# A mixture-of-experts stage whose first weight matrices are read per tile and whose second product is made of three fp32r products

## The chip, the cores and the metric

The kernel runs on one core of a Trainium2 chip. Work is done by five engines, each with an instruction queue of its own: TensorE (PE in the rows; its weight loads are PEld), VectorE (DVE), ScalarE (ACT), GpSimd (POOL) and SyncE (SP, which issues most DMAs). They meet through semaphores. The metric is the device time of one launch in microseconds; lower is better.

## What is computed

A pre-LN decoder layer on x of shape (8, 256, 256): attention with Gaussian scores, then cross-attention with 16 heads, then a mixture of eight experts, each added to x. Only the last part is touched:

```python
gate_logits = xs @ Wg                                   # xs: layernorm of x, (2048, 256)
weights, sel = jax.lax.top_k(gate_logits, 2)
weights = jax.nn.softmax(weights, axis=1)
h = jax.nn.relu(jnp.einsum('td,edf->etf', xs, W1) + b1[:, None, :])      # W1: (8, 256, 1024)
out_e = jnp.einsum('etf,efd->etd', h, W2) + b2[:, None, :]               # W2: (8, 1024, 256)
out = jnp.einsum('tk,tkd->td', weights, picked)         # the two chosen rows of out_e
```

## The kernel before

Each engine runs an order that is written out by hand. The attention part is a loop over the batches, software-pipelined: `attention` runs iterations -1 to 9, and in each of them the engines do pieces of up to four batches. Iterations 8 and 9 (`choosing` and `placing`) also route the first ten token tiles: `routing_table(0, 0..3)` builds in four rounds on VectorE the one-hot operands (`row_hot`, L1711, and three `tile_vals`, L1719) for the matmuls that make the table of slots, and `routing_index` turns the table into gather indices.

The expert part is a loop over 39 tiles of 128 slots, sorted by expert, in iterations n = 0 to 42, the first 18 unrolled. In iteration n GpSimd gathers the rows of tile n (L1876) and scatters tile n-4 into the output in HBM (L1890); TensorE transposes tile n-1 (`ex_rows_t`, L1901), makes the hidden layer of tile n-2 (`ex_hidden`, L1933, 16 fp32 matmuls, two records each) and the second product of tile n-3 (`ex_out`, L1966, 8 fp32 matmuls of 256 columns). ScalarE copies the transposed rows (L1907) and does four relus (L1952); VectorE copies W1 of the tile's expert out of the resident weights (`ex_weights`, L1918, 128x2048), does the other four relus (L1945), and adds the bias and multiplies by the routing weight (L1978, L1980). Each engine first reads the tile's expert from a table (`value_load`, L1852).

The first 13 tiles come from the first ten token tiles. The remaining six token tiles are routed on VectorE within iterations 3 to 12, after the tile's own work: the choice in 3, counts in 4, fillers and tile lists in 5, fillers and slots in 6, four table rounds in 7 to 10, and the index in 12. GpSimd can gather tile 13 (iteration 13) only after that index.

W1 and W2 of all experts, 16 MB, are kept in SBUF (`experts_w`). SP loads them expert by expert, one pair of 1 MB transfers after the other: expert 0 early, 1 in iteration 8, and from the fourth on after the last batch's heads are transposed (`p_hT`, L927).

Of the kernel before, what the change touches and what calls it, by code (L numbers as in the profile page):

```python
# [31 lines left out]
NB = 8  # L32
# [14 lines left out]
PLACE = KT * FF + FT * D  # L47
EARLY = 1
QROWS = 2 * 3 * HD
# [8 lines left out]
UNROLLED = 18  # L58

# [124 lines left out]
def run(core):  # L184
# [16 lines left out]
    for name, (engine, setup, finish) in programs.items():  # L201
        @engine
        def _(eng, name=name, setup=setup, finish=finish):
# [4 lines left out]
            if name != "sync":  # L208
                pipeline(eng, MAX_TILES, MOE_LAG, lambda it: experts(core, name, eng, it), first=UNROLLED)
# [15 lines left out]
def plan_memory(core):  # L225
# [22 lines left out]
    core.experts_w = buffer(core, "experts_w", [NE * PLACE])  # L248


def plan_shared(core):
    sb = partial(buffer, core)
    core.ident = sb("ident", [P])
    core.ones = sb("ones", [P])
    core.x2 = sb("x2", [TT, D])
# [5 lines left out]
    core.tile_loads = sb("tile_loads", [MAX_TILES + 1], I32)  # L261
# [76 lines left out]
def plan_late_experts(core, late_end):  # L338
    sb = partial(buffer, core)
    core.hid_t = [sb(f"hid_t{i}", [FT, P]) for i in range(2)]  # L340
# [74 lines left out]
    core.w1_now = [sb(f"w1_now{i}", [KT * FF]) for i in range(2)]  # L415
    end, core.cursor = core.cursor, start
# [16 lines left out]
def make_events(core):  # L433
# [3 lines left out]
    for n in "x_first0 x_first1 x_rest consts_first consts_in weights weights_value weights_cross weights_last mask_in experts_in experts_b residual_out".split():  # L437
        E[n] = sem(core, n)
# [20 lines left out]
    for n, k in per.items():  # L459
# [3 lines left out]
              "vec pool both filler filled prefix counted delta ex slots table tabled idx b1_in b1_t".split()}  # L463
    core.rows_in = RowsIn([sem(core, f"rows_in{i}") for i in range(4)])
    core.rows_out = dma_event(core, "rows_out")
    per = dict(gnow=1, snow=1, xT=1, slots_t=1, w1=1, hid=2, act_a=4, act_v=4, b1t=1,
# [239 lines left out]
def attention(core, name, eng, it):  # L706
# [14 lines left out]
    if name == "sync":  # L721
        if it.v == 1:
            for x in range(EARLY):
                load_expert(core, eng, x, core.E["experts_in"])
# [40 lines left out]
    exps(2, 2, 3, 4)  # L765
    at(0, st_rbf_out)
# [8 lines left out]
    exps(2, 8, 9)  # L775
    at(0, st_normalise, 1)
# [46 lines left out]
    at(2, st_transpose, "hT")  # L823
    scores(0, 0, 1, 2)
# [526 lines left out]
def store_residual(core, eng, b):  # L1351
    core.e["x2"].wait(eng, b)
    loads(core, eng, core.out.rearrange("b (t p) d -> b p t d", p=P)[b.v], x2_of(core, b), core.E["residual_out"])
# [41 lines left out]
def experts_sync(core, e):  # L1395
    t, r = core.t, core.r
    core.e["av"].wait(e, LAST_BATCH.back(1), 3)
    load_expert(core, e, EARLY, core.E["experts_in"])
# [9 lines left out]
def experts_rest_sync(core, e):  # L1408
    for x in range(EARLY + 1, NE):
        if x == EARLY + 2:  # L1410
            core.e["p_hT"].wait(e, LAST_BATCH)
        load_expert(core, e, x, core.E["experts_in"])


def load_expert(core, eng, x, sem):
    if x > 0:
        eng.wait_ge(sem, 32 * x)
    place = core.experts_w[:, (NE - 1 - x) * PLACE:(NE - x) * PLACE]
# [606 lines left out]
```

## Time and profile before

| | |
|---|---|
| median of 3 runs | 663.25 us (663.2 to 665.27) |
| profiled execution | 661.92 us, span 660.2 us |
| mean granted TensorE clock | 0.981 of full speed |
| PE busy | 613.9 us, 93% of the span |
| DVE, ACT, POOL busy | 395.3, 226.1 and 196.6 us |
| HBM read | 29.93 MB |

The span runs from the first to the last instruction of the profiled execution; the remaining 1.7 us of its time lie around it. Busy shares are means over stages that have different limits. The attention part fills the first 350 us, and the expert loop the rest.

### The profile page before, as it was taken

The numbers are of one execution on the slowest core, as the hardware profiler recorded it, in microseconds if no ns is written. First come the engines' busy times: TensorE is split into PE (matmuls) and PEld (weight loads), VectorE is DVE, ScalarE is ACT, GpSimd is POOL, SyncE is SP. The second block draws the span as 40 slices with busy tenths as digits, with TensorE's granted clock in tenths as the row PEclk, the third lists the DMA queues.
The fourth block names the chain that finished last, engine by engine and source line by source line (L and its number), as shares of the span: only waits on it lengthen the run. The fifth ranks groups of instructions, "written<-read, shape, count | busy, mean of one in ns | idle before, by whom it ended". The sixth has DMA issues, their size and how long they took to land.

```text
span 660.2 us, 14238 instructions
## 1 busy us (share of the span) xinstructions
PE 613.9 (93%) x4587; PEld 549.6 (83%) x4588; DVE 395.3 (60%) x1069; ACT 226.1 (34%) x537; POOL 196.6 (30%) x259
## 2 busy tenths in 40 slices
PE   4676999999999999998897999999999999999992
PEld 4576888888898988886676989999999999999992
DVE  4636848677686767676896477765344444544440
ACT  5332373645545373634252111112121221222120
POOL 8312120212012030101005134545345444444422
PEclk9979999999999999998989999999999999999997
DMA  7294818090642809082096883212222222222221
GB/s 219 93 147 120 89 23 92 2 125 23 76 72 37 110 5 141 3 92 71 7 338 200 256 252 96 33 26 48 42 33 32 38 41 32 33 38 40 32 25 16
DMA packets 46996, 52.80 MB, mean 80 GB/s; under 512 B 5920, under 2 KB 43648, under 8 KB 46944
## 3 DMA queue, kind: packets, MB, share of 16 engines
q1 hardware_dynamic: 37936, 41.08, 31.2%
q0 software_dynamic: 7616, 10.26, 9.9%
q10 hardware_dynamic: 1392, 0.79, 0.4%
q8 instruction: 30, 0.49, 0.3%
q14 instruction: 22, 0.18, 0.1%
HBM read 29.93 MB, written 9.31 MB: 59 GB/s over the span
## 4 chain that ended last, share of the span: by engine, by line
PE 80%; DVE 9%; DMA 3%; ACT 3%; issue 2%; POOL 1%; SPq 1%; DVEq 1%; POOLq 0%
PE bank L1933 20%; PE bank L1966 19%; PE bank L961 13%; PE bank L1287 4%; PE bank L1255 4%; PE bank L1198 4%; PE bank L1258 4%; PE bank L1201 4%; PE bank L927 2%; DMA q_stack<-cq_lo 1%; PE bank L1901 1%; PE bank L1097 1%; DMA exp_ring<-L_attn_Wo 1%; DVE row_max L1209 1%; DVE tile_vals L1719 1%
## 5 line engine op out<-in xcount | busy, mean ns | idle before, releaser
L1933 PE MATMUL bank<-slots_t,w_now 128*128 128x128 f32 x1248 | 146.0, 275 | 0.9 <-DVE w_now L1918 0.6
L1933 PEld LDWEIGHTS bank<-slots_t,w_now 128*128 128x128 f32 x1248 | 142.5, 192 | 1.6 <-DVE w_now L1918 1.6
L1966 PE MATMUL bank<-experts_w,hid_t 128*128 x624 | 141.2, 380 | 0.0
L1966 PEld LDWEIGHTS bank<-experts_w,hid_t 128*128 128x128 f32 x624 | 115.7, 190 | 14.1
L1890 POOL DMA_INDIRECT out<-y,scatter_now x39 | 70.8, 1816 | 137.2 <-DVE y L1980 121.2
L1952 ACT ACTIVATE hid_t<-bank,b_tile 128x128 f32<-128x128 f32 x156 | 44.6, 368 | 169.5 <-DVE b_tile L1939 169.5
L1209 DVE TENSOR_REDUCE row_max<-bank 128x2 f32<-128x512 f32 x128 | 81.1, 681 | 10.8 <-PE bank L1201 10.6
L1270 ACT ACTIVATE exp_ring<-bank 128x512 f32<-128x512 f32 x128 | 67.8, 605 | 30.1 <-PE bank L1258 30.0
L1918 DVE COPY w_now<-experts_w 128x2048 f32 x39 | 47.8, 1227 | 49.3 <-issue 41.5
L1201 PE MATMUL bank<-k_stack,q_stack 96*128 96x256 f32 x256 | 68.1, 380 | 0.0
L1258 PE MATMUL bank<-q_stack,k_stack 98*128 98x256 f32 x256 | 67.3, 383 | 0.0
L1978 DVE TENSOR_TENSOR y<-bank,b_row 128x256 f32<-128x256 f32 x39 | 16.5, 424 | 79.1 <-PE bank L1966 74.6
L1258 PEld LDWEIGHTS bank<-q_stack,k_stack 98*128 98x128 f32 x256 | 51.4, 201 | 3.6
L1201 PEld LDWEIGHTS bank<-k_stack,q_stack 96*128 96x128 f32 x256 | 50.7, 198 | 3.6
L1198 PE MATMUL bank<-mask_q,ident_bf 128*128 128x512 bf16 x128 | 50.3, 393 | 2.2 <-DMA q_stack<-cq_lo 2.2
L1255 PE MATMUL bank<-mask_k,ident_bf 128*128 128x512 bf16 x128 | 51.0, 398 | 0.0
L1876 POOL DMA_INDIRECT slots_in<-xn_rows,gather_now x39 | 42.7, 1095 | 26.5 <-POOL gather_now L1873 16.1
L860 POOL TENSOR_SCALAR rstd<-moments 128x2 f32<-128x2 f32 x24 | 5.9, 246 | 144.6 <-DVE moments L857 144.6
L1945 DVE TENSOR_SCALAR hid_t<-bank,b_tile 128x128 f32<-128x128 f32 x156 | 43.9, 344 | 7.9 <-DVE b_tile L1939 4.6
L1907 ACT ACTIVATE slots_t<-bank 128x256 f32<-128x256 f32 x39 | 15.0, 385 | 59.9 <-PE bank L1901 59.9
L1287 PE MATMUL bank<-exp_ring,v_aug 128*32 128x256 f32 x512 | 34.1, 385 | 0.0
L1873 POOL COPY gather_now<-gather_idx 128x1 uint32 x39 | 26.8, 687 | 15.5 <-DVE jump L1763 15.5
(266 smaller groups left out, 937.2 us busy)
## 6 DMA issues: line engine op xcount, KB each, us to landing
experts_w<-L_ffn_W SPq DMA_DIRECT2D x16, 1024.0 KB, 7.7
k_stack<-ck_hi SPq DMA_DIRECT2D x32, 128.0 KB, 4.7
q_stack<-cq_hi SPq DMA_DIRECT2D x32, 128.0 KB, 6.6
ctx_in<-ctx SPq DMA_DIRECT2D x8, 256.0 KB, 8.0
k_stack<-ck_lo SPq DMA_DIRECT2D x16, 128.0 KB, 4.6
q_stack<-cq_lo SPq DMA_DIRECT2D x16, 128.0 KB, 8.1
out<-x SPq DMA_DIRECT2D x7, 256.0 KB, 8.1
xn_rows<-xn_ffn SPq DMA_DIRECT2D x7, 256.0 KB, 8.1
```

The costliest lines, as they stand in the source:

```text
L961: mm = eng.matmul(out, a, b, start=start and i == 0, stop=stop and i == len(terms) - 1, skip_group_check=skip)
L1198: eng.matmul(ps[:, :], core.ident_bf[:, :], core.mask_q[:, :, :], start=True, stop=False, skip_group_check=True)
L1201: mm = eng.matmul(ps[:, qt * S:(qt + 1) * S], q_stack[0:QROWS, c, i, qt * P:(qt + 1) * P], k_stack[0:QROWS, i, :], start=False, stop=True, ...
L1209: core.e["maxed"].at(eng.tensor_reduce(core.row_max[:, :, h], ps[:, :].rearrange("p (t k) -> p t k", t=KT), AX.X, ALU.max))
L1255: eng.matmul(ps[:, :], core.ident_bf[:, :], core.mask_k[:, :, :], start=True, stop=False, skip_group_check=True)
L1258: mm = eng.matmul(ps[:, kt * S:(kt + 1) * S], core.k_stack[b.p][0:rows, i, kt * P:(kt + 1) * P], core.q_stack[b.p][0:rows, c, i, :], start ...
L1270: core.e["exp"].at(eng.activation(core.exp_ring[:, n % 8, :, :], ps[:, :], ACT.Exp, scale=HD ** -0.5))
L1287: mm = eng.matmul(ps[32 * q:32 * q + 32, (g % 2) * S:(g % 2 + 1) * S], core.v_aug[b.p][:, kt, head, :], core.exp_ring[:, head % 8, kt, :], ...
L1890: core.rows_out.at(eng.indirect_dma_start(core.out_rows, bass.IndirectOffsetOnAxis(ap=core.scatter_now[b.p][:, :], axis=0), core.y[b.p][:, ...
L1918: core.m["w1"].at(eng.tensor_copy(core.w1_now[b.p][:, :], core.experts_w[:, bass.ds(x * PLACE, KT * FF)]))
L1933: mm = eng.matmul(banks[half][:, f * P:(f + 1) * P], core.w1_now[b.p][:, start:start + P], core.slots_t[b.p][:, c, :], start=c == 0, stop= ...
L1966: mm = eng.matmul(ps[:, 0:D], core.hid_t[b.p][:, f, :], core.experts_w[:, bass.ds(x * PLACE + (KT * FF + f * D), D)], start=f == 0, stop=f ...
```

## The change

`experts_w` no longer holds W1. SP reads W1 of a tile's expert from HBM into one of two buffers (`ex_load`, 1 MB for each tile, from the place that the table names), after TensorE has finished the tile two before. VectorE's copy of W1 falls away, with its second `value_load`. W2 is kept as two parts, hi (rounded to fp32r) and lo (what the rounding left): for each expert ScalarE writes hi (128x2048) and then VectorE or GpSimd subtracts it from W2 to give lo (`split_expert`). GpSimd does experts 0 to 2, of which 1 and 2 lie in iteration 9 of the attention loop; VectorE does 3 to 7 in iterations 2 and 3 of the expert loop. ScalarE now does all eight relus of a tile into one fp32 buffer; VectorE parts the result into hid_hi (two copies of 128x512) and hid_lo (one subtraction of 128x1024). The second product is 24 fp32r matmuls: hi·hi, hi·lo, lo·hi. SP loads W2 with at most two transfers of 1 MB at a time, experts 3 to 6 after `p_hT` as before.

```diff
-PLACE = KT * FF + FT * D
+PLACE = 2 * FT * D
+POOL_SPLITS = 3
...
+    if placing and name in ("scalar", "gpsimd"):
+        split_expert(core, name, eng, 1)
     at(0, st_rbf_out)
...
     exps(2, 8, 9)
+    if placing and name in ("scalar", "gpsimd"):
+        split_expert(core, name, eng, 2)
...
+def split_expert(core, name, eng, x):
+
+    hi, lo = expert_part(core, x, 0), expert_part(core, x, 1)
+    if name == "scalar":
+        loaded(core, eng, x)
+        eng.activation(hi, lo.bitcast(F32), ACT.Copy).then_inc(core.w2["hi"], 1)
+        return
+    eng.wait_ge(core.w2["hi"], x + 1)
+    rest = eng.tensor_tensor(lo, lo.bitcast(F32), hi.bitcast(F32), ALU.subtract)
...
     elif name == "vector":
-        if n != 2:
-            at(1, ex_weights)
         if n == 1:
...
+        elif n == 2:
+            eng.wait_ge(core.w2["lo_pool"], POOL_SPLITS)
+            split_expert(core, name, eng, 3)
+        elif n == 3:
+            split_expert(core, name, eng, 4)
+            split_expert(core, name, eng, 5)
         at(2, ex_hidden)
+        if n == 3:
+            split_expert(core, name, eng, 6)
+            split_expert(core, name, eng, 7)
...
+def ex_load(core, name, eng, b):
+
+    core.m["hid"].wait(eng, b.back(2), apart=core.apart)
+    x = expert_of(core, eng, b)
+    rows = core.t["L0_ffn_W1"].rearrange("e (k p) n -> p e k n", p=P)
+    core.w1_in.at(eng.dma_start(core.w1_now[b.p][:, :, :].rearrange("p (e k) n -> p e k n", e=1),
+                                rows[:, bass.ds(x * -1 + (NE - 1), 1), :, :]), b)
...
         core.m["out"].wait(eng, b.back(2))
...
+        for half in range(2):
+            part = slice(half * half_tiles, (half + 1) * half_tiles)
+            core.m["h"].wait(eng, b, half)
+            core.m["hid_hi"].at(eng.tensor_copy(core.hid_hi[b.p][:, part, :], core.hid[:, part, :]))
+        core.m["hid_hi"].wait(eng, b)
+        core.m["hid_lo"].at(eng.tensor_tensor(core.hid_lo[b.p][:, :, :], core.hid[:, :, :],
+                                              core.hid_hi[b.p][:, :, :].bitcast(F32), ALU.subtract))
...
-        for f in range(FT):
-            mm = eng.matmul(ps[:, 0:D], core.hid_t[b.p][:, f, :],
-                            core.experts_w[:, bass.ds(x * PLACE + (KT * FF + f * D), D)],
-                            start=f == 0, stop=f == FT - 1)
+        for term, (left, part) in enumerate(((core.hid_hi, 0), (core.hid_hi, 1), (core.hid_lo, 0))):
+            if term == 2:
+                core.m["hid_lo"].wait(eng, b)
+            for f in range(FT):
+                mm = eng.matmul(ps[:, 0:D], left[b.p][:, f, :],
+                                core.experts_w[:, bass.ds(x * PLACE + (part * FT * D + f * D), D)],
+                                start=term == 0 and f == 0, stop=term == 2 and f == FT - 1)
```

On GpSimd, at the end of the attention loop, the program before goes from the last layernorm (rstd) straight to the gather of tile 0, which waits for the index (r_idx):

```order
L862 TENSOR_TENSOR rstd<-rstd,minus_half 128x2 [waits e_ln2_eps]
L1858 TENSOR_LOAD tile_col [waits xn_stored0,xn_stored1,r_idx]
L1858 ISA x2
L1873 ISA
L1873 COPY gather_now_152<-gather_idx_202 128x1
L1876 DMA slots_in_146<-xn_rows,gather_now_152 128x256 [waits m_gnow]
```

The changed program has there:

```order
L878 TENSOR_TENSOR rstd<-rstd,minus_half 128x2 [waits e_ln2_eps]
L1463 TENSOR_TENSOR experts_w<-experts_w 128x2048 [waits w2_hi] x2
L1923 TENSOR_LOAD tile_col [waits xn_stored0,xn_stored1,r_idx]
L1923 ISA x2
L1938 ISA
L1938 COPY gather_now_152<-gather_idx_202 128x1
```

Two subtractions of 128x2048, experts 1 and 2, have come in ahead of the gathers; on VectorE the third and fourth table rounds stand at this time.

On VectorE, iterations 2 and 3 of the expert loop, the program before copies W1, does the relus of tile 1 and goes on to y of tile 0 and the routing of the last batch (logits, MAX):

```order
L1918 COPY w_now_211<-experts_w 128x2048
L1852 TENSOR_LOAD tile_expert
L1852 ISA x2
L1939 ISA
L1939 COPY b_tile_151<-b_cols 128x8
L1945 TENSOR_SCALAR hid_t_133<-bank,b_tile_151 128x128 [waits m_hid,m_b1t]
L1945 TENSOR_SCALAR hid_t_133<-bank,b_tile_151 128x128 x3
```

The changed program has, from the hidden layer of tile 0 to y of tile 0:

```order
L2018 CAST hid_hi_132<-hid 128x512 [waits m_h] x2
L2020 TENSOR_TENSOR hid_lo_212<-hid,hid_hi_132 128x1024 [waits m_hid_hi]
L1463 TENSOR_TENSOR experts_w<-experts_w 128x2048 [waits w2_hi] x2
L1917 TENSOR_LOAD tile_expert
L1917 ISA x2
L2013 ISA
L2013 COPY b_tile_151<-b_cols 128x8
L2018 CAST hid_hi_133<-hid 128x512 [waits m_h] x2
L2020 TENSOR_TENSOR hid_lo_213<-hid,hid_hi_133 128x1024 [waits m_hid_hi]
L1463 TENSOR_TENSOR experts_w<-experts_w 128x2048 [waits w2_hi] x2
L1917 TENSOR_LOAD tile_expert
L1917 ISA x2
```

Four of the five subtractions that VectorE has (the fifth stands ahead of tile 0's copies) have come between the tiles' own work and the routing of the last batch.

## Rows read from the trace of the kernel before

**Rows 1.** Busy time in windows, expert stage: five engines, clock, DMA share, GB/s
```profile
438.00:640.00 202.00, 202.00 (x1394) 189.11 (x1393) 92.27 (x236) 42.42 (x140) 88.98 (x108) 1.00 0.23 36
```

**Rows 2.** Chain that ended last, two tiles late on: start us, us, what
```profile
572.41 0.22 PE bank L1901 x2
572.63 3.57 PE bank L1933 x32
```

**Rows 3.** The same chain where tile 11's second product ends
```profile
452.99 3.46 PE bank L1966 x16
```

**Rows 4.** The same chain in attention, fp32r products, 128x256 moving
```profile
155.54 1.42 PE bank L961 x12
...
178.41 2.74 PE bank L961 x24
```

**Rows 5.** Groups by form, VectorE: count | busy us, mean ns | idle before
```profile
L1918 DVE COPY w_now<-experts_w 128x2048 f32 x39 | 47.8, 1227 | 49.3 <-issue 41.5 <-PE bank L1933 7.8
...
L1123 DVE TENSOR_TENSOR p_lo<-prob,p_hi 128x512 fp32r<-128x512 f32 x8 | 5.5, 685 | 5.8 <-ACT p_hi L1116 5.8
...
L1588 DVE TENSOR_TENSOR filler<-iota_f,filler_row 128x1024 f32<-128x1024 f32 x2 | 2.4, 1218 | 0.0
```

**Rows 6.** Timeline of all engines near 24 us: start us, us, engine, instruction
```profile
23.88 1.27 POOL L888 TENSOR_TENSOR x<-x,bias_attn_bo 128x512 f32<-128x512 f32 x1 [6.10 <-DVE bias_attn_bo L671]
24.24 1.45 DVE L611 TENSOR_TENSOR xattnWvl<-exp_ring,xattnWvh 128x512 fp32r<-128x512 f32 x1
...
25.62 0.68 DVE L611 TENSOR_TENSOR xattnWol<-exp_ring,xattnWoh 128x512 fp32r<-128x512 f32 x1
```

**Rows 7.** Groups by form, GpSimd
```profile
L1016 POOL TENSOR_TENSOR q_sq<-q_sq 128x256 f32<-128x256 f32 x8 | 5.9, 732 | 69.8 <-ACT q_sq L1012 69.8
```

**Rows 8.** Timeline of all engines, the end of the attention loop
```profile
334.29 2.76 ACT L1270 ACTIVATE exp_ring<-bank 128x512 f32<-128x512 f32 x5 [0.28 <-PE bank L1258]
...
338.14 0.73 DVE L880 TENSOR_SCALAR xn_ffn<-x,moments,rstd 128x256 f32<-128x256 f32 x2
...
343.05 1.55 DVE L1719 TENSOR_TENSOR tile_vals<-onehot,local_vals 128x400 fp32r<-128x400 f32 x3
```

**Rows 9.** Chain that ended last: last batch's heads are transposed
```profile
350.50 0.66 PE bank L927 x4
```

**Rows 10.** Timeline of VectorE, iterations 6 and 7 of the expert loop
```profile
393.16 1.23 DVE L1918 COPY w_now<-experts_w 128x2048 f32 x1 [1.27 <-issue]
...
396.52 0.35 DVE L1980 TENSOR_SCALAR y<-y,slot_weight 128x256 f32<-128x256 f32 x1 [0.16 <-DVE y L1978]
...
406.62 1.50 DVE L1719 TENSOR_TENSOR tile_vals<-onehot,local_vals 128x384 fp32r<-128x384 f32 x3
408.08 1.23 DVE L1918 COPY w_now<-experts_w 128x2048 f32 x1
```

**Rows 11.** Timeline of ScalarE, one tile's first four relus
```profile
562.62 1.14 ACT L1952 ACTIVATE hid_t<-bank,b_tile 128x128 f32<-128x128 f32 x4 [3.99 <-DVE b_tile L1939]
```

**Rows 12.** Windows cut at five routing pieces on VectorE (columns as Rows 1)
```profile
378.45:381.65 3.20, 3.20 (x26) 3.07 (x25) 2.80 (x19) 0.00 (x0) 2.05 (x3) 1.00 0.91 283
386.79:391.90 5.11, 5.11 (x39) 4.87 (x38) 4.74 (x23) 0.00 (x0) 3.51 (x4) 1.00 0.87 233
396.79:399.80 3.01, 3.01 (x29) 2.98 (x28) 2.87 (x16) 0.00 (x0) 2.05 (x2) 1.00 0.81 269
412.50:415.06 2.56, 2.56 (x26) 2.56 (x25) 2.52 (x10) 0.00 (x0) 1.72 (x2) 1.00 0.00 0
439.64:442.43 2.79, 2.79 (x17) 2.48 (x16) 2.58 (x12) 0.22 (x1) 0.00 (x0) 1.00 0.08 11
```

**Rows 13.** Timeline of GpSimd: gather of tile 13 after the index
```profile
443.92 1.03 POOL L1876 DMA_INDIRECT slots_in<-xn_rows,gather_now  x1 [0.59 <-POOL gather_now L1873]
```

**Rows 14.** DMA issues: KB each, median us from issue to landing
```profile
experts_w<-L_ffn_W SPq DMA_DIRECT2D x16, 1024.0 KB, 7.7
...
slots_in<-xn_rows,gather_now POOLq DMA_INDIRECT x39, 2.9
```

More of the change, by code:

```diff
@@ L58 @@
 UNROLLED = 18
+EARLY_BATCHES = 6
 class Step:
@@ L339, in plan_late_experts @@
     sb = partial(buffer, core)
-    core.hid_t = [sb(f"hid_t{i}", [FT, P]) for i in range(2)]
+    core.hid_hi = [sb(f"hid_hi{i}", [FT, P], F32R) for i in range(2)]
     core.y = [sb(f"y{i}", [D]) for i in range(2)]
@@ L462, in make_events @@
     core.r = {n: sem(core, "r_" + n) for n in
-              "vec pool both filler filled prefix counted delta ex slots table tabled idx b1_in b1_t".split()}
+              "vec pool both filler filled prefix counted delta ex slots table tabled idx b1_in b1_t order".split()}
+    core.w2_in = [sem(core, f"w2_in{i}") for i in range(2)]
+    core.w2 = {n: sem(core, "w2_" + n) for n in "hi lo lo_pool".split()}
+    core.w1_in = dma_event(core, "w1_in")
     core.rows_in = RowsIn([sem(core, f"rows_in{i}") for i in range(4)])
     core.rows_out = dma_event(core, "rows_out")
-    per = dict(gnow=1, snow=1, xT=1, slots_t=1, w1=1, hid=2, act_a=4, act_v=4, b1t=1,
+    per = dict(gnow=1, snow=1, xT=1, slots_t=1, hid=2, h=2, hid_hi=2, hid_lo=1, b1t=1,
                out=1, y=2)
@@ L823, in attention @@
     at(2, st_transpose, "hT")
+    if it.v == 2 and name in ("scalar", "gpsimd"):
+        split_expert(core, name, eng, 0)
     scores(0, 0, 1, 2)
@@ L1397, in experts_sync @@
     core.e["av"].wait(e, LAST_BATCH.back(1), 3)
-    load_expert(core, e, EARLY, core.E["experts_in"])
+    for x in range(EARLY, POOL_SPLITS):
+        load_expert(core, e, x)
     memory_over(core, e)
@@ L1934, in ex_hidden @@
                                     core.slots_t[b.p][:, c, :], start=c == 0, stop=c == KT - 1)
             core.m["hid"].at(mm)
+    elif name == "scalar":
+        core.m["b1t"].wait(eng, b)
+        core.m["hid_lo"].wait(eng, b.back(1))
+        for half in range(2):
+            core.m["hid"].wait(eng, b, half)
+            for f in range(half_tiles):
+                g = half * half_tiles + f
+                act = eng.activation(core.hid[:, g, :], banks[half][:, f * P:(f + 1) * P],
+                                     ACT.Relu, bias=core.b1_tile[b.p][:, g:g + 1])
+            core.m["h"].at(act)
```

127 lines of the change are left out of this document (71 added, 56 removed).

## Prediction

> **What bounds the kernel now.** I read the busy time in windows first, then the chain of work that ended last. From 438 to 640 us TensorE is busy 202.0 of 202.0 us at full clock [rows 1], and the chain there is TensorE alone: two transposes 0.22, the hidden layer 3.57 [rows 2], the second product 3.46 [rows 3], so 7.25 us for a tile. What is saved on TensorE there counts in full. Before about 440 us it is otherwise: VectorE has the routing of the last six token tiles beside each tile's work, and TensorE waits for it. So there are two stretches, with opposite signs for this change: the early one, where VectorE is late and gets more to do, and the late one, where TensorE gets less.
>
> **The late stretch.** The second product becomes 24 fp32r matmuls of 256 columns. In attention, 24 such took 2.74 us, 114 ns each, and 12 took 1.42, 118 ns [rows 4]. Sixteen of the new ones have a register instruction ahead of them, so I take 117 ns: 2.80 us. Period: 0.22 + 3.57 + 2.80 = 6.59, a gain of 0.66 us for a tile (0.72 at 114 ns, 0.60 at 119). From the end of tile 11's second product to that of tile 38 there are 27 periods: 17.7 us (16 to 19.4).
>
> What must stay hidden for that: **W1's load.** Its buffer is free when the hidden layer two tiles before ends, and wanted two periods less 3.57 us later, 9.6 us. Ahead of it stand a value load, 0.64 us (two of them cost the 1.27 us ahead of a W1 copy [rows 10]), and the issue, at most the 1.03 us that GpSimd's indirect one takes [rows 13]; landing took 7.7 us in the median, two transfers at a time [rows 14]. It is hidden, by 0.2 us at that landing and by more alone. **VectorE and ScalarE.** One round of theirs without routing, from y of one tile to y of the next: value load 0.64, bias copy and wait 0.3, eight relus at the pace of 4 in 1.14 us, 2.2 [rows 11], wait 0.1, the second copy to hid_hi, wait 0.15, the subtraction with two value loads behind it 1.4, y 0.93 (0.42 by the same route, wait 0.16, 0.35 [rows 10]). The copy is f32 to fp32r, 128x512, which no row shows: the 128x2048 copy took 1227 ns, so a quarter of its length is some 0.43 with its fixed part, and a 128x512 subtraction 0.685 [rows 5]; below is the copy's pace, above the subtraction's. I take 0.45, since it is a copy. The round is 6.2 us, 6.4 at the upper end: just under 6.59, so TensorE stays the bound by little. ScalarE's own sum, 2.2 + 0.4, is no bound.
>
> **The early stretch, step by step.** *The attention loop's end.* GpSimd gets two subtractions of 128x2048. Its 128x512 took 1.27 us [rows 6] and its 128x256 0.73 [rows 7], so 2.1 ns an element and 4.6 us for one. What else they cost is seen near 24 us: VectorE's 128x512 subtraction, both inputs in SBUF, took 1.45 us beside GpSimd's, and its twin just after it 0.68; it ended 0.54 us after GpSimd's (25.69 against 25.15), as if it had begun only then [rows 6]. So such an operation of VectorE stands still while GpSimd's runs. The Trainium skill has this as a rule ("SBUF — State Buffer", section "Who interferes with whom"): a VectorE instruction with two SBUF inputs and a GpSimd one that reads SBUF need the same port pair, and who starts first holds it for the whole instruction. By that rule each subtraction here blocks for its full length; were the block never longer than the row's 0.8 us, the two would cost under 2 us.
>
> ScalarE's five exps from 334.29 on are followed, after the third, by its part for expert 1 (five of 512 elements take 2.76 us, so 2048 elements some 2.1 us) [rows 8]. GpSimd begins at about 338.3. VectorE then has the last layernorm scaling and two table rounds left, from 338.14 to 344.60, 6.5 us [rows 8], nearly all operations of that kind, and the table products, the index and the gathers stand behind them. If VectorE wins the port between GpSimd's two, the tables end at 338.3 + 4.6 + 6.5 = 349.4, 4.8 us late; if GpSimd goes twice, 9.4 late. Nothing decides between them; I take **7**, from 1 (only ScalarE's delay) to 9.4. Expert 0's split, in attention iteration 2, can block VectorE in the same way; at up to 4.6 us, with most of VectorE's work there from PSUM, I take **1**.
>
> *The first tiles.* Experts 3 and 4 are fetched when the last batch's heads are transposed, at 351.2 before [rows 9], so at 358.2 (with the 7). Landing: the first of two, 5.3 us, between a gather's 2.9 and 7.7 [rows 14]: 363.5. ScalarE's hi 2.1: 365.6. VectorE's lo: 1218 ns at 1024 elements and 685 at 512 [rows 5], 1.04 ns an element, so 2.3 at 2048: 368.0. Only then come bias and relus of tile 0 (3.1: 371.1) and its two parts (1.8: 372.9). Expert 4's hi runs on ScalarE behind these relus, 5's behind the stores and the next transposed rows, to 377.2; VectorE's lo 5 ends at 379.5, relus and parts of tile 1 at 384.5, 6 and 7 at 389.4, y of tile 0 at 390.6, the choice at 392.3.
>
> *The rounds with routing.* Added to a round of 6.2 are 3.2, 5.1 and 3.0 us in iterations 4 to 6 and 2.56 in each of 7 to 10 [rows 12]. After a table the value load is hidden (the next operation starts at once, at 408.08 behind 1.50 us from 406.62 [rows 10]), so 5.55 there. Iterations 4 to 11: 4 x 6.2 + 4 x 5.55 + 11.3 + 10.2 = 68.5, to 460.8. In 12, the round up to hid_lo 5.1 and the index 2.8 [rows 12]: 468.7. The gather of tile 13 was issued 1.5 us behind the index (443.92 against 442.43 [rows 12, 13]) and lands 2.9 later [rows 14], with up to 1 us for the issue itself: 473.5. Then transposes, hidden layer of tile 12, second product of tile 11: 6.6, to 480.1. Before it ended at 452.99 + 3.46 = 456.45 [rows 3], so **23.6 us late**, with expert 0's 1 us 24.6.
>
> **Sum.** 24.6 - 17.7 = +6.9 us. The profiled execution would go from 661.92 to 668.8; the median of the runs shown is 1.3 us higher, so I forecast 670.
>
> Bounds of the loss: the port 1 and 0 in place of 7 and 1 (-7), landing 2.9 or 7.7 (-2.4, +2.4), relus and copies at the upper end (+0.25 in some ten rounds, +2.5), port at its worst (+2.4 and +3.6).
>
> **Rivals.**
> - *The port costs nothing.* VectorE's short operations slip in between, or GpSimd's two fall into its waits; only ScalarE's 1 us stays. Against it stands the 1.45 us row. 24.6 - 7 = 17.6 us lost, 17.7 gained: 663, no change.
> - *The rounds overlap better, the faster end.* The loss hangs on ten rounds of 6.2 us in a row. Where relus begin on the first half of a hidden layer while value loads run behind y, a round is 5.3: 9 us less, and the port at its lower case 4.8 (2.2 less): 24.6 - 11.2 - 17.7 = -4.3, so 659. It decides from rounds under some 5.5 us on. For it: value loads do hide behind long operations. Against: the bias copy stands between y and the relus in VectorE's order, and ScalarE waits for it.
> - *VectorE and ScalarE become the bound of the late stretch.* At relus of 2.5, copies of 0.685 and a value load of 0.8, the round is 6.95: the gain falls to 27 x 0.3 = 8, the loss grows by 7: 670 + 9.7 + 7 = 687. From 6.6 on it is the bound, only 0.4 above my sum.
> - *W1's stream is late.* If landing beside the gathers and scatters takes 9.2 us, a period is (0.64 + 1.03 + 9.2 + 3.57) / 2 = 7.2, no gain at all: 670 + 17.7 = 688. The DMA engines moved 36 GB/s there [rows 1]; 1 MB for each 6.59 us adds 159. With one such transfer at a time I hold it unlikely.
>
> **Chances.** Forecast (slower, the port costs 4 to 10 us) 0.52; port free 0.17, within 0.3%; better overlap 0.13, faster; VectorE's round as bound 0.13; W1 late 0.05. What a measurement of this kernel can tell from no change is about 0.3%, 2 us. Slower 0.70, same 0.17, faster 0.13. The range leaves out the W1 case and the worst of the round's case, and reaches at the lower end to the better overlap: 659 to 683; the likeliest's own range is 665 to 677.
>
> **What would show it.** The second product in 2.7 to 2.9 us and a late period near 6.6, TensorE busy without a gap there; two GpSimd subtractions of about 4.6 us near 338 to 350 with VectorE's table operations lengthened beside them; the choice of the last batch some 20 us later than before; a gap on TensorE ahead of tile 13's transposes; end of tile 11's second product near 480. Wrong would be: tables that run on beside GpSimd, rounds of VectorE under 5.5 or over 6.6 us, a copy to hid_hi far from 0.45, or a hidden layer that waits for W1.

## The result and the profile after

The changed kernel takes 674.18 us in the median of four runs (672.43 to 675.65), the kernel before 663.24 (663.2 to 665.27): ratio 1.0156, 95% interval 1.0121 to 1.0191, so 11 us slower, where 670 was forecast with a range of 659 to 683. The profiled execution took 675.28 us with a span of 672.3, 12.1 more than before.

**The late stretch.** First the windows of the changed kernel (columns as in rows 1), then the chain that ended last, one tile of it:

```profile
345.00:353.00 8.00, 0.60 (x7) 0.36 (x3) 7.96 (x10) 2.16 (x5) 5.21 (x2) 0.69 0.10 33
353.00:358.00 5.00, 4.79 (x18) 4.25 (x19) 3.01 (x9) 1.79 (x3) 0.00 (x0) 0.50 0.63 210
...
360.00:440.00 80.00, 66.66 (x505) 64.63 (x498) 50.82 (x142) 29.77 (x75) 24.90 (x33) 0.87 0.65 202
...
476.10:482.10 6.00, 6.00 (x33) 6.00 (x33) 2.09 (x5) 1.52 (x5) 3.50 (x5) 0.58 0.32 49
...
480.00:640.00 160.00, 160.00 (x1400) 160.00 (x1400) 72.83 (x144) 61.88 (x217) 85.39 (x97) 1.00 0.71 197
```

```profile
570.88 0.22 PE bank L1967 x2
571.10 3.57 PE bank L1997 x32
574.67 2.83 PE bank L2041 x24
```

From 480 to 640 us TensorE is busy throughout and at full clock, as before [rows 1], and its chain has three terms again: transposes 0.22, hidden layer 3.57 as in [rows 2], and the second product 2.83 where [rows 3] had 3.46. The period is 6.62 instead of 7.25. W1's stream is there, 197 GB/s instead of 36, and TensorE never waits for it. From the end of tile 11's second product to the end of the span it took 660.2 - 456.45 = 203.75 us before and takes 672.3 - 484.97 = 187.33 now: 16.4 us won.

**The early stretch** loses more than that. The same chain, from the end of the attention loop to tile 13:

```profile
341.24 9.12 DVE xn_ffn L896 x2
...
364.03 5.66 DMA experts_w<-L_ffn_W
369.71 7.65 DMA experts_w<-L_ffn_W
377.38 10.61 DMA experts_w<-L_ffn_W
388.01 1.92 ACT experts_w L1460
...
394.47 0.22 DVE both L1566
...
471.51 3.86 DMA slots_in<-xn_rows,gather_now
...
476.10 6.04 PE bank L1997 x32
482.14 2.83 PE bank L2041 x24
```

Four places are to be seen. The last layernorm scaling of VectorE, 0.73 us in [rows 8], takes 9.12. Then three landings of W2 stand one behind the other, 24 us, until ScalarE has expert 7. The choice of the last batch (`both`) ends at 394.7. And TensorE waits for tile 13's gather; the hidden layer right behind that wait takes 6.04 us instead of 3.57, at a granted clock of 0.58 in its window, between the levels of 1.2 and 2.4 GHz. Tile 11's second product ends at 484.97, 28.5 us later than in [rows 3]: 12.9 us are there when the last batch's heads are transposed (364.0 against 351.2), 10.2 come between that and the choice, and 5.4 behind it.

The rounds of the expert loop themselves lost nothing. In the kernel before TensorE was the bound already from about 404 us on, table rounds and all (windows as in rows 1):

```profile
404.00:438.00 34.00, 34.00 (x240) 32.20 (x239) 24.54 (x69) 6.38 (x21) 17.79 (x17) 1.00 0.20 32
```

A round with a table took 7.77 us there (hidden layers begin at 411.62 and 419.39 in its chain). In the change it takes 7.63, and VectorE and ScalarE set it, so the saving on TensorE shows there only in part.

What stands beside the scaling, in the timeline of GpSimd and VectorE (start us, us, engine, instruction):

```profile
341.05 9.16 POOL L1463 TENSOR_TENSOR experts_w<-experts_w 128x2048 fp32r<-128x2048 f32 x2 [0.81 <-ACT experts_w L1460]
341.16 9.20 DVE L896 TENSOR_SCALAR xn_ffn<-x,moments,rstd 128x256 f32<-128x256 f32 x2
```

Two VectorE operations start 0.1 us after GpSimd's two subtractions and end 0.15 us after them. Taken one by one, in narrower windows of the same timeline, each scaling ends 0.15 us after one subtraction (the first subtraction ends at 345.71, the second at 350.21):

```profile
341.16 4.70 DVE L896 TENSOR_SCALAR xn_ffn<-x,moments,rstd 128x256 f32<-128x256 f32 x1
...
345.78 4.58 DVE L896 TENSOR_SCALAR xn_ffn<-x,moments,rstd 128x256 f32<-128x256 f32 x1
```

So VectorE does get a turn between the two, for one operation; the next one meets the second subtraction.

The prices of the new operations, in groups by form (count | busy us, mean ns | idle before):

```profile
L1460 ACT ACTIVATE experts_w<-experts_w 128x2048 fp32r<-128x2048 f32 x8 | 15.5, 1939 | 1.2 <-DMA experts_w<-L_ffn_W 1.2
L1463 POOL TENSOR_TENSOR experts_w<-experts_w 128x2048 fp32r<-128x2048 f32 x3 | 13.7, 4596 | 9.6 <-ACT experts_w L1460 9.6
L1463 DVE TENSOR_TENSOR experts_w<-experts_w 128x2048 fp32r<-128x2048 f32 x5 | 11.5, 2291 | 0.8 <-ACT experts_w L1460 0.6
...
L2018 DVE CAST hid_hi<-hid 128x512 fp32r<-128x512 f32 x78 | 33.6, 431 | 77.7 <-ACT hid L2007 59.7
```

And the gathers' row among the DMA issues, a median of 6.7 us to landing where [rows 14] had 2.9:

```profile
slots_in<-xn_rows,gather_now POOLq DMA_INDIRECT x39, 6.7
```

### The profile page after: what moved, and what is told of

It is laid out like the page before. It is cut to its first block, busy times and chain, and to the rows that moved or that the text cites. A ratio compares the mean times of both kernels' runs of the same rounds, so it can differ in the third digit from the quotient of the medians.

```text
span 672.3 us, 15234 instructions
## 1 busy us (share of the span) xinstructions
PE 604.3 (90%) x4857; PEld 556.9 (83%) x4900; DVE 407.6 (61%) x994; ACT 281.2 (42%) x701; POOL 213.3 (32%) x262
## 4 chain that ended last, share of the span: by engine, by line
PE 67%; DVE 12%; DMA 8%; issue 4%; ACT 4%; SPq 2%; DVEq 2%; POOL 1%; POOLq 0%
PE bank L1997 15%; PE bank L977 13%; PE bank L2041 13%; PE bank L1217 5%; PE bank L1274 4%; PE bank L1303 4%; DMA experts_w<-L_ffn_W 4%; PE bank L1271 3%; PE bank L1214 3%; DMA q_stack<-cq_lo 2%; ACT hid L2007 2%; PE bank L943 2%; DVE xn_ffn L896 1%; DMA exp_ring<-L_attn_Wo 1%; PE bank L1113 1%
## 5 line engine op out<-in xcount | busy, mean ns | idle before, releaser
L2007 ACT ACTIVATE hid<-bank,b_tile 128x128 f32<-128x128 f32 x312 | 85.7, 376 | 124.1 <-DVE b_tile L2013 100.3
L1956 POOL DMA_INDIRECT out<-y,scatter_now x39 | 63.0, 1615 | 133.1 <-DVE y L2055 125.9
L2041 PE MATMUL bank<-experts_w,hid_hi 128*128 x624 | 85.8, 291 | 0.5 <-issue 0.5
L2018 DVE CAST hid_hi<-hid 128x512 fp32r<-128x512 f32 x78 | 33.6, 431 | 77.7 <-ACT hid L2007 59.7
L2041 PEld LDWEIGHTS bank<-experts_w,hid_hi 128*128 128x128 f32 x624 | 78.7, 194 | 0.6 <-issue 0.6
L2020 DVE TENSOR_TENSOR hid_lo<-hid,hid_hi 128x1024 fp32r<-128x1024 f32 x39 | 47.8, 1225 | 1.3
L1271 PE MATMUL bank<-mask_k,ident_bf 128*128 128x512 bf16 x113 | 45.7, 404 | 0.0
L2041 PE MATMUL bank<-experts_w,hid_lo 128*128 x312 | 44.5, 286 | 0.0
L2041 PEld LDWEIGHTS bank<-experts_w,hid_lo 128*128 128x128 f32 x312 | 41.0, 195 | 0.0
L1214 PE MATMUL bank<-mask_q,ident_bf 128*128 128x512 bf16 x101 | 39.6, 392 | 0.0
L1938 POOL COPY gather_now<-gather_idx 128x1 uint32 x39 | 29.6, 759 | 16.2 <-DVE jump L1805 16.1
```

The costliest lines, as they stand in the source:

```text
L1214: eng.matmul(ps[:, :], core.ident_bf[:, :], core.mask_q[:, :, :], start=True, stop=False, skip_group_check=True)
L1271: eng.matmul(ps[:, :], core.ident_bf[:, :], core.mask_k[:, :, :], start=True, stop=False, skip_group_check=True)
L1956: core.rows_out.at(eng.indirect_dma_start(core.out_rows, bass.IndirectOffsetOnAxis(ap=core.scatter_now[b.p][:, :], axis=0), core.y[b.p][:, ...
L2007: act = eng.activation(core.hid[:, g, :], banks[half][:, f * P:(f + 1) * P], ACT.Relu, bias=core.b1_tile[b.p][:, g:g + 1])
L2041: mm = eng.matmul(ps[:, 0:D], left[b.p][:, f, :], core.experts_w[:, bass.ds(x * PLACE + (part * FT * D + f * D), D)], start=term == 0 and ...
```

## The experiments

The theory: the late stretch gains what was forecast; the loss comes from work that was put ahead of other work in engines that go in order (GpSimd's two subtractions ahead of the tables, by way of VectorE; the splits of W2 ahead of the last batch's choice; the choice's lateness then reaches tile 13). Rivals: the W1 stream itself slows the rest by its traffic; VectorE has simply more to do before the index, wherever it stands. "Less than the change" below is a difference of medians from different sets of runs. The kernel before, run again in each set, had 664.4 us beside the first four experiments, 663.37 beside the next four and 664.08 beside the last two, where it had 663.24 beside the change; so such a difference holds to about 1 us, and the ratio to the kernel before is the better measure.

**Are GpSimd's subtractions the port term?** In `split_expert` those of experts 1 and 2 are cut to eight columns.

```diff
     eng.wait_ge(core.w2["hi"], x + 1)
+    if name == "gpsimd" and x > 0:
+        hi, lo = hi[:, 0:8], lo[:, 0:8]
```

> The changed kernel, but GpSimd's two subtractions near the end of the attention loop work on 8 of their 2048 columns (the low parts of W2 of experts 1 and 2 are left as loaded, for the rest). Theory, the port: VectorE's layernorm scaling, 9.20 us for the pair in the changed kernel, returns to about 0.73 us, the table rounds end some 8.5 us earlier, and everything behind follows: 674.2 - 8.5 = 665.7 us (664 to 667). Rival, the stream: it is W1's and W2's transfers that make the early stretch late; then the scaling still ends earlier, but the tiles wait for the same landings and the time stays within 2 us of 674. Rival, the clock: TensorE's waits halve its clock; a shorter wait then gives more than 8.5, 10 to 12 us.

Measured: 663.72 us (662.52 to 665.9), ratio to before 0.9994 (0.9981 to 1.0008), 10.5 less than the change. In its chain the scaling is short again and the tables follow at once, but the W2 landings still stand in a row:

```profile
339.35 0.65 DVE xn_ffn L896 x2
...
352.32 5.71 DMA experts_w<-L_ffn_W
358.05 7.93 DMA experts_w<-L_ffn_W
365.99 10.76 DMA experts_w<-L_ffn_W
```

The last batch's heads are transposed 11.7 us earlier than in the change (end at 352.32 against 364.03), and nearly all of it reaches the end. What follows: these two instructions cost about 10 us, more than the port's 8.5, and in the range of the rival with the clock. The profiles part it: 1.9 of the 11.7 us are there at GpSimd's last `rstd`, ahead of the subtractions (336.66 against 338.56), 8.5 come up to the end of the last table operation, and 1.4 behind it, where TensorE works at a granted clock of 0.50 in the change and its last five table products take 1.07 us instead of 0.84.

**Does it help to move them?** GpSimd does them behind its first four gathers instead.

```diff
-    if placing and name in ("scalar", "gpsimd"):
+    if placing and name == "scalar":
         split_expert(core, name, eng, 1)
...
                 ex_gather(core, name, eng, Step(b // 2, b % 2))
+            split_expert(core, name, eng, 1)
+            split_expert(core, name, eng, 2)
```

> The changed kernel, but GpSimd does its subtractions for experts 1 and 2 after the first four gathers; ScalarE's parts stay where they are, and nothing is left out. Theory, the port: VectorE's tables are free (-8.5 us), but the subtractions (9.2 us) now run beside the last batch's layernorm, which they block for up to one subtraction, and VectorE's first own subtraction waits for them until about 364 to 366 where it could start near 362: some 3 us are lost again, so 674.2 - 5.5 = 668.7 us (666 to 671). Rival, the stream: no change, 672 to 676. If GpSimd were the bound there anyway: 674 or more.

Measured: 667.69 us (665.93 to 669.03), ratio 1.0047 (1.0031 to 1.0063), 6.5 less than the change. The timelines of GpSimd and VectorE show where the rest went:

```profile
355.23 8.98 POOL L1463 TENSOR_TENSOR experts_w<-experts_w 128x2048 fp32r<-128x2048 f32 x2
364.19 0.23 POOL L876 TENSOR_SCALAR rstd<-moments 128x2 f32<-128x2 f32 x1
...
365.27 0.73 DVE L896 TENSOR_SCALAR xn_ffn<-x,moments,rstd 128x256 f32<-128x256 f32 x2 [8.18 <-POOL rstd L878]
```

No operation of VectorE is stretched now, but the last batch's `rstd`, queued behind the subtractions on GpSimd, lets VectorE wait 8.18 us. The block by the port became a wait in GpSimd's queue.

**Tile 13's index one piece earlier.** The index stands ahead of the hidden parts of iteration 12, not behind them.

```diff
+        if n == 12:
+            routing_index(core, eng, 1)
         at(2, ex_hidden)
...
-        if n == 12:
-            routing_index(core, eng, 1)
```

> The changed kernel, but in iteration 12 VectorE makes the index before the hidden layer of tile 10 and not behind it. Theory, the gather: tile 13's gather starts some 5 us earlier, TensorE's wait of 3.4 us ahead of its transposes goes, and so does the hidden layer of 6.0 us at the low clock behind it (3.57 otherwise): 674.2 - 6 = 668.2 us (667 to 670). Rival, VectorE's sum alone sets the end of this stretch: the index costs the same 2.8 us in either place, no change, 673 to 675.

Measured: 668.45 us (666.43 to 671.37), ratio 1.0056 (1.0037 to 1.0075), 5.7 less than the change. TensorE goes through without the gap (the second product ahead of this row ends at 471.4):

```profile
471.48 3.74 PE L1997 MATMUL bank<-slots_t,w_now 128*128 128x128 f32 x32
```

The hidden layer behind the gather takes 3.74 us in this view, where the change's took 6.25 in the same view (6.04 in the chain): the wait of 3.4 us had cost itself and another 2.5.

**Is that 2.5 the clock?** 28 transposes of the identity fill TensorE's wait ahead of tile 13's rows.

```diff
+        if isinstance(b.v, int) and b.v == FIRST:
+            core.m["slots_t"].wait(eng, b.back(1))
+            for _ in range(28):
+                eng.transpose(ps[:, 0:P], core.ident[:, :], core.ident[:, :])
         core.rows_in.wait(eng, b)
```

> The changed kernel, but TensorE fills its wait ahead of tile 13's transposes with 28 transposes of the identity (some 3.1 us) into a bank that is overwritten next. Theory, the clock: the granted clock was low behind the wait (hidden layer of tile 12 in 6.04 us against 3.57); with work in the wait it stays high and the hidden layer takes 3.6: 674.2 - 2.4 = 671.8 us. Rival: the low clock comes from the stretch as a whole, not from this wait; then the hidden layer is still near 6 us, no change.

Measured: 673.3 us (670.91 to 673.79), ratio 1.0122 (1.0097 to 1.0148), 0.9 less than the change (2.0 less where each is taken against the kernel before of its own set), where 2.4 were expected. The times don't part this from no change; the profile does.

```profile
471.55 3.22 PE L1967 MATMUL bank<-ident 128*128 128x128 f32 x28
476.55 0.44 PE L1971 MATMUL bank<-ident,slots_in 128*128 128x128 f32 x2 [1.78 <-DMA slots_in<-xn_rows,gather_now]
476.82 3.74 PE L2001 MATMUL bank<-slots_t,w_now 128*128 128x128 f32 x32
```

```profile
476.80:480.50 3.70, 3.70 (x35) 3.70 (x34) 1.31 (x4) 1.53 (x5) 1.90 (x2) 1.00 0.10 30
```

The granted clock of that stretch is 1.00 now and the hidden layer is at its usual length, so its 2.5 us were the clock behind a wait in which TensorE did nothing; but the gather landed 1.1 us later in this profile than in the change's, and that ate part of it.

**The stream alone.** W1 is streamed, the second product is the fp32 one again, and the relus are shared as before; the splits and their waits stay in place, each cut to eight columns.

```diff
-        eng.activation(hi, lo.bitcast(F32), ACT.Copy).then_inc(core.w2["hi"], 1)
+        eng.activation(hi[:, 0:8], lo[:, 0:8], ACT.Copy).then_inc(core.w2["hi"], 1)
...
-    rest = eng.tensor_tensor(lo, lo.bitcast(F32), hi.bitcast(F32), ALU.subtract)
+    rest = eng.tensor_copy(hi[:, 8:16], lo[:, 8:16])
...
+        for f in range(FT):
+            mm = eng.matmul(ps[:, 0:D], core.hid_t[b.p][:, f, :],
+                            core.experts_w[:, bass.ds(x * PLACE + (FT * D + f * D), D)],
+                            start=f == 0, stop=f == FT - 1)
```

> One part of the change alone: W1 is read per tile as in the changed kernel, but the second product stays the eight fp32 matmuls on W2 as loaded, with the relus shared by ScalarE and VectorE as before; the splits are left as operations on 8 columns that nothing uses. Theory, the splits and rounds are what costs, and the stream is hidden: the late period stays at 7.25 us, and the early rounds lose VectorE's W1 copy (1.23 us) and a value load (0.64 us) in iterations 4 to 6: 663.2 - 5.6 = 658 us (655 to 661). Rival, the stream: gathers that took 2.9 us before and 6.7 in the changed kernel, and W2's later landings, make tiles wait: 664 us or more.

Measured: 673.28 us (672.27 to 674.73), ratio 1.0151 (1.0125 to 1.0177): 15 us over the 658 expected, and on the side of the rival. The theory as I had it missed here. The chain:

```profile
352.41 6.25 DMA experts_w<-L_ffn_W
358.68 8.94 DMA experts_w<-L_ffn_W
367.63 9.94 DMA experts_w<-L_ffn_W
...
377.83 0.17 DVE experts_w L1463
...
381.64 0.21 DVE both L1566
```

The heads are transposed 1.2 us later than in [rows 9], and the splits have no length, yet the choice (`both`) ends at 381.85, 10.3 later than the 371.59 of the same operation in the trace before. VectorE and ScalarE wait in order for W2 of expert 7, in iteration 3, ahead of y of tile 0 and the choice. So the landings of W2, waited for at that place, cost 9 us with no split work at all. And of the 5.6 us that VectorE's lost W1 copy was to give back, only 1 came: from the choice to the end of tile 11's second product it is 83.7 us (381.85 to 465.54) against 84.9 before, since TensorE bounded these rounds already.

**W1 loaded for tiles 0 and 1 only**; all other tiles use what these two loads left.

```diff
-        if n is None or n >= 2:
-            at(0, ex_load)
         if n == 2:
+            core.m["hid"].wait(eng, Step(0, 0))
             load_expert(core, eng, NE - 1)
...
-        core.w1_in.wait(eng, b)
+        if isinstance(b.v, int) and b.v < 2:
+            core.w1_in.wait(eng, b)
```

> The changed kernel, but W1 is read for tiles 0 and 1 alone; later tiles use what lies in the two buffers (their hidden layers are of the wrong expert). Theory: the stream costs little: the wait of 3.1 us ahead of tile 2's hidden layer is beside VectorE's splits, W2 of expert 7 lands some us earlier but VectorE is there only 2 us later, and tile 13's gather lands 1 us earlier: 674.2 - 3 = 671 us (669 to 674), the late period 6.62 as it is. Rival, the stream: 8 us or more are gained, 666 or less.

Measured: 670.51 us (668.52 to 671.82), ratio 1.0109 (1.0083 to 1.0134), 3.7 less than the change. Not all of that need be the stream's: in the two profiles 2.1 us of difference are there at GpSimd's last `rstd` in attention (336.51 against 338.56), where no W1 load has been left out yet. The W2 landings no longer stand in a row in its chain; ScalarE's and VectorE's splits do, and the time from the heads to the prefix product is nearly the same (391.61 - 361.31 = 30.3 against 394.82 - 364.01 = 30.8). Landings and splits lie beside each other, and either of them fills this stretch. Nor are the W2 landings shorter without W1 beside them: those of experts 3 to 7 took 5.8 to 9.9 us here, and the three in the change's chain 5.66 to 10.61.

Its profile shows the port with another operation first. Timeline of GpSimd and VectorE:

```profile
338.17 9.73 POOL L1463 TENSOR_TENSOR experts_w<-experts_w 128x2048 fp32r<-128x2048 f32 x2
...
337.65 5.86 DVE L1761 TENSOR_TENSOR tile_vals<-onehot,local_vals 128x400 fp32r<-128x400 f32 x3
343.43 4.94 DVE L896 TENSOR_SCALAR xn_ffn<-x,moments,rstd 128x256 f32<-128x256 f32 x2
```

Here a table operation waits for the first subtraction and a scaling for the second (GpSimd's pair takes 9.73, not 9.16). The table operations are 4.31 us over their 1.55, the scaling 4.21 over its 0.73: 8.5 in sum, the same as the 8.5 of the two scalings in the change.

**Two of the three products.** The term from the hidden layer's low part is left out.

```diff
-        for term, (left, part) in enumerate(((core.hid_hi, 0), (core.hid_hi, 1), (core.hid_lo, 0))):
+        for term, (left, part) in enumerate(((core.hid_hi, 0), (core.hid_hi, 1))):
...
-                                start=term == 0 and f == 0, stop=term == 2 and f == FT - 1)
+                                start=term == 0 and f == 0, stop=term == 1 and f == FT - 1)
```

> The changed kernel without the third term of the second product (16 matmuls; hid_lo is still made and used by nothing). TensorE's own sum for a late tile falls from 6.62 to 5.69 us. Theory, VectorE and ScalarE are close behind TensorE: a table round of 7.65 us less 2.56 and with a value load of 0.64 not hidden is 5.7, so the late period is 5.7 to 6.2 with gaps on TensorE, and the time 674.2 less 27 times 0.4 to 0.9: 656 us (650 to 663). Rival, there is ample room: period 5.69 with no gap, 27 times 0.93 less: 649 us or below.

Measured: 664.32 us (663.03 to 665.82 in nine runs, 1118.18 in the tenth), ratio 1.0014 (0.9998 to 1.0029), just over the upper end of what was expected. TensorE's chain would be 5.7 us for a tile, but VectorE's timeline repeats every 6.3 to 6.5:

```profile
560.50 0.17 DVE L2013 COPY b_tile<-b_cols 128x8 f32 x1 [0.57 <-issue]
561.97 0.43 DVE L2018 CAST hid_hi<-hid 128x512 fp32r<-128x512 f32 x1 [1.29 <-ACT hid L2007]
...
567.04 0.17 DVE L2013 COPY b_tile<-b_cols 128x8 f32 x1 [0.99 <-issue]
```

This is the round of VectorE and ScalarE, from one tile's bias to the next: 6.54, and 6.26 for the tile behind it. It stands in the chain from 509 to 585 us, and lies right under TensorE's 6.62. It is not all that is missing: two gathers stand in the same chain ahead of that and behind it (6.58 us from 487.09, 5.36 from 589.29), and TensorE waited for gathers 9.3 us in ten waits between 480 and 640.

**Order alone.** All of the change's work stays, at full length; only its places move. GpSimd does the two subtractions after the index and ahead of the first gathers, with the last batch's moments ahead of the third; TensorE instead of VectorE waits for GpSimd's splits; the index stands early as above; and VectorE copies a tile's b1 columns right behind y of the tile before (`ex_bias`).

```diff
+            split_expert(core, name, eng, 1)
+            split_expert(core, name, eng, 2)
...
+            at(1, ex_bias)
...
-            eng.wait_ge(core.w2["lo_pool"], POOL_SPLITS)
...
+        if n == 12:
+            routing_index(core, eng, 1)
...
```

> The changed kernel with all its work, in another order: GpSimd's two subtractions stand between the index and the first gathers; the index of iteration 12 stands ahead of the hidden layer; and VectorE copies a tile's bias right behind y of the tile two before it, ahead of the routing pieces, so that ScalarE's relus run beside them. Theory: port -9, tile 13's stall -6, and some 1.8 us of VectorE's wait for relus in each of the rounds 3 to 9, of which W2's landings take some back, -8: 674.2 - 23 = 651 us (647 to 658), faster than both kernels. Rival, the stream or W2's landings set the early end: only the port's and the stall's part, or less: 660 to 668.

Measured: 658.69 us (656.39 to 660.04), ratio 0.9915 (0.9884 to 0.9947): faster than both kernels, though 8 us over what was expected and just under the rival's range. GpSimd's 9.02 us now hold up the first gathers, and TensorE starts tile 0 late:

```profile
347.27 9.02 POOL L1463 TENSOR_TENSOR experts_w<-experts_w 128x2048 fp32r<-128x2048 f32 x2 [9.77 <-DVE jump L1805]
...
353.98 2.34 DVE L1993 COPY b_tile<-b_cols 128x8 f32 x1 [0.72 <-issue]
...
387.84 0.23 DVE L1566 TENSOR_TENSOR both<-onehot 128x48 f32<-128x48 f32 x1
```

Even a copy of 128x8, 0.17 us elsewhere, takes 2.34 beside it. The choice starts at 387.84, still behind the splits.

**The bias copy alone**: the change with only `ex_bias` moved, as in the edit above (`at(1, ex_bias)`).

> The change with one move on VectorE: the copy of b1's columns for the next tile stands right behind y instead of ahead of the hidden high parts one iteration later, so that ScalarE's relus find it ready; nothing else moves. Theory (the round of VectorE and ScalarE, 7.6 us beside the tables, carries a value load and a copy of some 0.5 us between y and the relus): about 0.4 to 0.5 us less in each of ten rounds, so the index and tile 13 come 4 to 5 us earlier: 674.2 - 4.5 = 670 (668 to 671.5); late period unchanged at 6.62. Rival (ScalarE waits for TensorE's hidden layer in these rounds anyway, the copy is hidden): 674, no change against the change.

Measured: 671.76 us (669.37 to 673.52), ratio 1.0095 (1.0062 to 1.0129), 2.4 less than the change (3.3 where each is taken against the kernel before of its own set); between theory and rival. In the table rounds of the change, ScalarE's relus begin every 7.63 us, each time behind the bias copy, which stands behind VectorE's table:

```profile
442.48 2.17 ACT L2007 ACTIVATE hid<-bank,b_tile 128x128 f32<-128x128 f32 x8 [4.57 <-DVE b_tile L2013]
...
450.11 2.17 ACT L2007 ACTIVATE hid<-bank,b_tile 128x128 f32<-128x128 f32 x8 [5.03 <-DVE b_tile L2013]
```

With the copy early they wait for TensorE, which with its table product needs 7.16 (second half of the relus in the same view):

```profile
446.75 1.14 ACT L2016 ACTIVATE hid<-bank,b_tile 128x128 f32<-128x128 f32 x4 [0.56 <-PE bank L2006]
...
453.91 1.14 ACT L2016 ACTIVATE hid<-bank,b_tile 128x128 f32<-128x128 f32 x4 [0.56 <-PE bank L2006]
```

That is some 0.5 us for a round with a table, and the rounds with fillers ahead of them gain more (y of one tile to y three tiles on: 29.5 us in the change, 25.4 here). From the end of the choice to the end of `scatter_idx` it is 70.2 us instead of 75.1: the 4 to 5 us of the theory. They don't all arrive: in this profile the choice ended 1.5 us later (396.2), and tile 13's gather took 5.65 us in the chain instead of 3.86, so that tile 11's second product ends only 2.7 us earlier, at 482.31.

**The choice first.** From the reordered kernel: each of GpSimd's subtractions behind two gathers, the choice ahead of the splits of experts 4 to 7, and these one in each of the iterations 3 to 6.

```diff
+            split_expert(core, name, eng, n + 1)
...
-        elif n == 2:
-            split_expert(core, name, eng, 3)
-        elif n == 3:
-            split_expert(core, name, eng, 4)
-            split_expert(core, name, eng, 5)
...
+        if n in (3, 4, 5, 6):
+            split_expert(core, name, eng, n + 1)
```

> From the version called reordered: GpSimd issues the gathers of tiles 0 and 1 ahead of its subtraction for expert 1, and those of tiles 2 and 3 ahead of that for expert 2; VectorE has y of tile 0, the router, the best two and the choice of the last batch ahead of the splits of experts 4 to 7, which stand one each at the ends of iterations 3 to 6 (ScalarE's parts behind the relus of iterations 2 to 5); TensorE waits before the second product of tile k for the splits of expert k (no expert is without a tile here). Theory (subtractions that stand ahead of what others wait for are the loss, not their length): hidden layer of tile 0 ends near 359 instead of 370.8, the choice near 375 instead of 387.8, the splits of 4 to 7 then add 2.3 in each of four rounds: index about 5 us earlier than in reordered: 653 (649 to 657). Rival (VectorE's sum of work up to the index is the bound, order is indifferent): 658.7, as reordered.

Measured: 650.83 us (649.11 to 652.97), ratio 0.9788 (0.974 to 0.9837): 2% faster than the kernel before and 23 us under the change, with the same operations on the data. Two of its windows:

```profile
360.00:440.00 80.00, 74.01 (x606) 73.22 (x606) 63.48 (x164) 35.26 (x97) 47.85 (x42) 0.95 0.67 202
440.00:480.00 40.00, 40.00 (x351) 39.96 (x350) 20.36 (x48) 15.98 (x54) 22.71 (x24) 1.00 0.71 197
```

TensorE is busy 74.01 us of the 80 in which the change had 66.66, and no W2 landing stands in its chain from 344 us on. The last batch's counts (L1506) are on TensorE at 381, against 395 in the change. The hidden layer of tile 0 ended later than I had expected (at 364.3 instead of 359), since the gathers still waited for the index and for their landing. This run moves several things at once (the subtractions, the choice, TensorE's waits, on top of the order above); how the 8 us against the reordered kernel divide among them is not shown.

## Why the prediction was right in sign, and where its sizes were off

**The late stretch: right.** The second product was 2.83 (2.80 forecast), the period 6.62 (6.59), the gain 16.4 (17.7). The copy to hid_hi took 431 ns where 0.45 was chosen between bounds of 0.43 and 0.685; at 0.685 the second of them alone, the one that stands in the round, would have put the round at 6.5 to 6.8 (an estimate from these rows), about TensorE's 6.62. The round was forecast at 6.2 and measured at 6.26 to 6.54 in the kernel with two terms. W1 was hidden there; it was waited for once, 3.11 us in the profile of the change, ahead of tile 2's hidden layer.

**The early stretch: 28.5 us late, where 24.6 was the sum.** Step by step:

- *The port, "I take 7".* It cost 8.5. The step that failed is the sentence that if VectorE wins the port between GpSimd's two, the tables end 4.8 us late. VectorE did win a turn between them, in the change and in the kernel with two W1 loads, but for one operation only, and the next met the second subtraction: both lengths are paid either way. The rule of the Trainium skill ("SBUF — State Buffer", section "Who interferes with whom"), that who starts first holds the shared port for the whole instruction, agrees: the two scalings took 4.70 and 4.58 us beside subtractions of 4.66 and 4.55. The rival in which the port costs nothing is out.
- *What stands behind the port.* The last batch's heads were transposed at 364.0, 12.9 later than in [rows 9]; 7 was carried forward and 1 for expert 0's split. The 12.9 are 3.0 ahead of the port, 8.5 for it and 1.4 behind it. TensorE, busy for 0.60 us from 345 to 353, then worked at a granted clock of 0.50, the level of 1.2 GHz, until 358: the last two sets of five table products took 1.42 and 1.07 us in its chain, the last one 0.84 with short subtractions. The 3.0 us are there at GpSimd's `rstd` near 91 us (91.45 against 88.48), ahead of the first split, and no larger at the one near 159 us, behind it: expert 0's split, taken at 1, cost nothing that shows. At the last `rstd` they are 0.3 to 3.2 us from profile to profile (reordered the least); their cause stays open.
- *From the heads to the choice* 34.1 us were forecast (358.2 to 392.3) and 30.7 measured. The sum was about right, but by the wrong chain: "the first of two, 5.3 us" counted one landing and let ScalarE's and VectorE's splits run from there. In the trace the landings of experts 3 to 7 form a chain of three (5.66, 7.65, 10.61), since SP has at most two W2 transfers in flight; and ScalarE waits only 0.69 us for the last of them, so close do the splits run beside it. The kernel that only streams shows these landings costing 9 us with no split work at all; the kernel without the stream shows the split work filling the same time. Either would have done.
- *The rounds with tables* were 7.63, not 8.1. The prediction also read the kernel before wrongly here: it says that before about 440 us TensorE waits for VectorE, and from 404 us on TensorE was busy throughout.
- *From the choice to tile 11's end* 87.8 us were forecast and 90.3 measured. Up to the index it was 1.1 less; the gather's issue and landing took 0.6 more, and TensorE's work behind it 3.0 more, 2.5 of them the hidden layer at low clock behind the wait for tile 13, which the prediction did not have.

That the sum came within 4 us of the loss is in part luck: 4.9 too little up to the heads, 3.4 too much from there to the choice, 2.5 too little behind it.

**The other rivals.** Better overlap of the rounds did not come by itself: ScalarE waited for the bias copy, as the prediction said against it. VectorE as the bound of the late stretch missed by 0.1 to 0.4 us a tile. W1's stream late: excluded late, and about 3.7 us in all, of which a part need not be its own.

**Where the gain went.** It was there and was given back in front. Most of the loss was order: two instructions on a shared port, waits for W2 and its splits ahead of the routing, and with them the wait for tile 13, which an index one piece earlier takes away. A small copy behind a long one kept the rounds from giving more. With these moved, what stays of the 28.5 us is 4.8 (tile 11's second product ends at 461.26 in the last kernel, 456.45 before), and the gain of the late stretch, 16.2 there, shows. The 4.8 are 8.7 still missing at the end of the choice (380.25 against 371.59), less what the shorter rounds behind it gain.

## What to carry to other kernels

When a change adds work in two engines, cost it where it stands in each in-order queue, not by its length: what is queued behind it, who waits for that, and whether the two engines can run at the same time at all. A wait for a transfer costs what stands behind the waiting instruction, even where the work it guards is nil; so put work that feeds a long dependency chain (here routing) ahead of preparation that is needed only tiles later, and spread the latter. A saving on the engine that bounds one stretch is safe only if the other stretch, with another bound, has room for what pays for it. And ask which engine bounds a round before a term is booked as saved there: VectorE's W1 copy gave back almost nothing, since TensorE bounded those rounds.

## What the runs showed of the hardware that was not expected

- Two GpSimd subtractions of 128x2048, 9.16 us, held scalings of VectorE, a table operation and even a copy of 128x8, each until the subtraction beside it ended. Between the two VectorE got one operation through, and that saved it nothing: 8.5 us were lost with two scalings beside them as with a table operation and a scaling (1.55 + 9.20 against 5.86 + 4.94).
- Behind TensorE's wait for tile 13, 3.40 us, the hidden layer took 6.25 us instead of 3.74, at a granted clock of 0.58; transposes of the identity in that wait undid it.
- With W1 streaming, the gather's median landing went from 2.9 to 6.7 us (3.3 with two W1 loads alone), while the late stretch was not slowed by it.
- The table products behind TensorE's other wait, 7.61 us for VectorE's operands, ran at a granted clock of 0.50. A wait of TensorE cost more than its own length at both places, 1.4 us here and 2.5 there.
